# The sort back to edge order in 16-bit keys, in a graph layer with gated experts on one Trainium2 core

## The chip, the core and the metric

The kernel is one program on one core of a Trainium2 chip. The metric is the device's time for one execution, in microseconds. The engines are named as in the profile: PE (matmuls; PEld its weight loads), DVE (the vector engine), ACT (activations), POOL (here mostly the issuing of indirect DMAs), SP (issues the other DMAs).

## What is computed

The part of the reference that matters here, with the rest in a line each:

```
# x: 12500 x 256; src: 212500 edges in order of dst; edge_attr: 212500 x 32
time_feat = relu(edge_attr @ W_time.T + b_time)          # 64 features an edge
sums   = segment_sum(time_feat, src, num_segments=n)
counts = segment_sum(ones, src, num_segments=n)
node_time_feat = sums / maximum(counts, 1)[:, None]
fused = relu(concatenate([node_feat, node_time_feat]) @ W_fusion.T + b_fusion)
x = x + xn + fused @ W_up.T + b_up      # xn = layernorm(x)
x = x + ffn(layernorm(x))      # a shared MLP and the best two of four experts
```

The sums over edges by `src` are the irregular part: the edges come in the order of another index.

## The kernel before

The edges, padded to 212,992, are cut into groups of 256 (`G`), a group into 2 tiles of 128. 104 groups (`GROUPS_A_SET`) make a set, 8 sets the whole. Nodes lie in 49 buckets of 256. The main loop has 208 steps of 4 groups each. In a step PE computes the features of the step's edges (line 670), takes off with ACT's help their bf16 parts (lines 688 and 1592), and moves each group's rows with six matmuls against a one-hot matrix (line 684) into the order of the buckets, three rows of one bucket to a block. ACT copies the blocks into one of nine row buffers (line 1598), and POOL scatters them with an indirect DMA into a table in DRAM (line 1798), four in a step. A row buffer is free again when its scatter has landed. The one-hot matrix is made on DVE by line 1330 from `codes`, which give each edge of a group its slot; three buffers let DVE run ahead. When a part of the table is full (a quarter of the sets), SP loads it back, DVE makes one-hots of the nodes (line 1212), PE sums (line 713) and DVE adds to `sums` (line 1232); for the first three parts this runs in later steps of the loop, for the last after it. Then the dense layers follow for all nodes.

The slot of an edge is found by a sort on DVE. It is done for 104 groups at a time, one group a partition, and for the sets of `SETS_OF_SORT = (1, 1, 2, 2, 2)` side by side: sorts 0 and 1 have one set, sorts 2, 3 and 4 two. `sort_step(b, i)` writes step `i` of sort `b`. The first pass is a sorting network of 36 stages (`NST`) over 16-bit keys, the bucket in the upper eight bits and the edge's place in the group in the lower. Each stage is two instructions of `exchange` (lines 1130 and 1131). The middle part (`MIDDLE`, lines 1150 to 1188) finds with two scans a set each key's rank in its bucket, `turn` = rank mod 3, and the row, a count of up to `RG` = 118. The second pass is the same network over 32-bit floats, place x 1024 + turn x RG + row, and brings the edges back to their order. The last step (line 1194) takes the place off; what is left is the code:

```
elif i < SORT_STEPS - 1:
    q = i - NST - len(MIDDLE)
    exchange(q, v(f[q % 2]), v(f[(q + 1) % 2]), n)
else:
    after_op()
    op(e.tensor_tensor(v(t[0]), v(f[NST % 2]), b3d(idx_key, G, n), ALU.subtract))
```

PE transposes the codes (line 661, `turn_codes`) and ACT writes them out (line 1604). `after_op` waits until all earlier instructions of the sort have finished.

Sort 0 runs ahead of the loop, from 8.35 us on, each of its steps in turn with a bucket count (line 1106) or a step of the sizes (`size_step`, lines 913 to 1028). The other four run inside the loop: `sort_windows` gives the steps, (1, 20), (22, 46), (51, 98) and (103, 150), and `sort_at` spreads the sort's steps over them by work numbers (`NARROW_WORK`, `MIDDLE_WORK`, `WIDE_WORK`, `LAST_WORK`). In a step of the loop DVE's stream has a turn of the table, then the one-hots of the next step (lines 1322 and 1330), statistics of nodes (lines 1361 to 1375), the sort's steps and the counts.

## Time and profile before

| | |
|---|---|
| median of 3 runs | 2190.01 us (2188.02 to 2191.96) |
| the profiled execution, its own time | 2190.82 us |
| its span in the profile | 2189.0 us |
| PE busy | 2015.0 us (92%) |
| DVE busy | 1743.9 us (80%) |
| ACT busy | 1314.0 us (60%) |
| POOL busy | 1133.9 us (52%) |
| granted clock of PE over the span | 0.97 |

The span is the time from the first to the last instruction on the core. A DVE instruction's record overlaps the start of the next one by some 0.08 us, so what an instruction takes of the stream is read from start to start. The loop's first one-hot starts at 64.91 us, the first scatter at 69.6, the last at 1383.2.

### The profile page before, as it was taken

The numbers are of one execution on the slowest core, as the hardware profiler recorded it, in microseconds if no ns is written. First come the engines' busy times: TensorE is split into PE (matmuls) and PEld (weight loads), VectorE is DVE, ScalarE is ACT, GpSimd is POOL, SyncE is SP. The second block draws the span as 40 slices with busy tenths as digits, with TensorE's granted clock in tenths as the row PEclk, the third lists the DMA queues.
The fourth block names the chain that finished last, engine by engine and source line by source line (L and its number), as shares of the span: only waits on it lengthen the run. The fifth ranks groups of instructions, "written<-read, shape, count | busy, mean of one in ns | idle before, by whom it ended". The sixth has DMA issues, their size and how long they took to land.

```text
span 2189.0 us, 74658 instructions
## 1 busy us (share of the span) xinstructions
PE 2015.0 (92%) x26946; PEld 1684.2 (77%) x26946; DVE 1743.9 (80%) x5353; ACT 1314.0 (60%) x2811; POOL 1133.9 (52%) x915
## 2 busy tenths in 40 slices
PE   4789888899999899999999999687879999999998
PEld 1577676798889799999899999677756766666666
DVE  9888998888887799998687777588976776767675
ACT  2588788888788777778877787100014444444443
POOL 0587888778887878887777777200011111111110
PEclk7799999999999999999999999899989999999999
DMA  2244334676676677777678877577741121211111
GB/s 84 73 123 129 124 122 127 186 210 195 195 205 178 179 221 212 215 217 218 187 223 235 251 222 206 160 192 197 205 118 44 44 65 44 65 44 64 46 51 33
DMA packets 239404, 323.63 MB, mean 148 GB/s; under 512 B 42144, under 2 KB 213965, under 8 KB 238706
## 3 DMA queue, kind: packets, MB, share of 16 engines
q1 hardware_dynamic: 176564, 192.90, 33.4%
q0 software_dynamic: 41504, 103.41, 13.1%
q10 hardware_dynamic: 20970, 22.54, 3.8%
q8 instruction: 218, 3.57, 0.7%
q14 instruction: 148, 1.21, 0.2%
HBM read 186.34 MB, written 175.77 MB: 165 GB/s over the span
## 4 chain that ended last, share of the span: by engine, by line
PE 68%; DVE 10%; DMA 7%; ACT 6%; issue 5%; SPq 2%; DVEq 1%; POOL 1%; ACTq 1%; POOLq 0%
PE moved L684 15%; PE bank L713 14%; PE bank L800 9%; PE bank L670 7%; PE moved L813 7%; PE bank L688 4%; DMA arena<-table 3%; DMA table<-arena 3%; PE bank L840 2%; ACT arena L1598 2%; DVE arena L1130 2%; DVE arena L1330 2%; ACT arena L1592 2%; PE bank L697 1%; DVE arena L1131 1%
## 5 line engine op out<-in xcount | busy, mean ns | idle before, releaser
L1798 POOL DMA_INDIRECT table<-arena x832 | 1035.0, 1244 | 328.5 <-issue 267.4
L1598 ACT ACTIVATE arena<-moved 128x588 bf16<-128x588 f32 x832 | 546.5, 662 | 150.9 <-PE moved L684 120.6
L684 PE MATMUL moved<-arena 128*128 128x196 bf16 x4992 | 593.6, 255 | 7.0 <-ACT arena L1598 6.1
L684 PEld LDWEIGHTS moved<-arena 128*128 128x128 f16 x4992 | 455.3, 98 | 82.7 <-ACT arena L1598 18.8
L1592 ACT ACTIVATE arena<-bank 128x512 f32<-128x512 f32 x624 | 372.4, 597 | 151.5 <-PE bank L670 134.1
L1232 DVE TENSOR_TENSOR sums<-sums,bank 128x130 f32 x816 | 231.6, 284 | 156.2 <-PE bank L713 136.3
L1330 DVE TENSOR_TENSOR arena<-arena 128x2832 f16<-128x2832 f16 x208 | 338.0, 1625 | 18.0 <-PE moved L684 11.2
L713 PE MATMUL bank<-arena 128*128 128x64 bf16 (+1 forms) x7344 | 277.6, 193 | 31.9 <-DVE sums L1232 16.7
L713 PE MATMUL bank<-arena,w_all 128*128 128x64 bf16 (+1 forms) x7344 | 280.3, 194 | 19.5 <-DVE sums L1232 15.6
L713 PEld LDWEIGHTS bank<-arena 128*128 128x128 bf16 x7344 | 258.6, 98 | 36.7 <-DVE arena L1212 31.0
L713 PEld LDWEIGHTS bank<-arena,w_all 128*128 128x128 bf16 x7344 | 261.1, 98 | 24.4 <-DVE w_all L1212 17.7
L1700 ACT ACTIVATE arena<-bank,w_all 128x512 f32<-128x512 f32 (+1 forms) x225 | 152.6, 679 | 206.3 <-PE bank L800 115.5
L1212 DVE TENSOR_TENSOR arena<-arena 128x768 bf16<-128x768 bf16 x408 | 224.3, 551 | 30.4 <-DMA arena<-table 29.8
L1814 POOL TENSOR_TENSOR arena<-arena 128x4 f32<-128x4 f32 (+1 forms) x25 | 25.2, 1006 | 423.6 <-DVE arena L1503 423.6
L670 PE MATMUL bank<-w_all,arena 97*128 97x192 f32 (+1 forms) x1248 | 235.7, 326 | 4.6 <-ACT arena L1592 3.7
L1212 DVE TENSOR_TENSOR w_all<-arena 128x768 bf16<-128x768 bf16 x408 | 224.1, 551 | 10.6 <-DMA arena<-table 9.8
L800 PE MATMUL bank<-held,w_high 128*128 128x512 f32 (+1 forms) x600 | 221.0, 418 | 0.9 <-ACT arena L1700 0.5
L670 PEld LDWEIGHTS bank<-w_all,arena 97*128 97x128 f32 x1248 | 201.2, 193 | 6.7 <-issue 4.7
L688 PE MATMUL bank<-arena,minus_ident 128*128 128x512 bf16 x416 | 170.7, 410 | 38.2 <-ACT arena L1592 37.6
L1805 POOL TENSOR_TENSOR arena<-arena,w_all 128x1024 f32<-128x1024 f32 (+1 forms) x25 | 57.6, 2303 | 270.8 <-DMA arena<-x_ln 234.3
L1713 ACT ACTIVATE arena<-bank 128x256 f32<-128x256 f32 x25 | 9.4, 376 | 236.7 <-PE bank L827 236.7
L813 PE MATMUL moved<-w_all,arena 128*128 128x256 f32 x588 | 142.2, 384 | 0.0
(287 smaller groups left out, 2652.1 us busy)
## 6 DMA issues: line engine op xcount, KB each, us to landing
arena<-table SPq DMA_DIRECT2D x672, 147.0 KB
arena<-in_attr SPq DMA_DIRECT2D x208, 144.0 KB
arena<-table ACTq DMA_DIRECT2D x144, 147.0 KB
table<-arena POOLq DMA_INDIRECT x832
x_ln<-arena SPq DMA_DIRECT2D x98, 128.0 KB
arena<-in_x SPq DMA_DIRECT2D x97, 128.0 KB
arena<-x_ln SPq DMA_DIRECT2D x24, 512.0 KB, 4.7
out_rows<-arena SPq DMA_DIRECT2D x24, 512.0 KB, 3.2
```

What stands on the lines that cost most here:

```text
L670: mm = e.matmul(bank[ZB][:, q * 3 * A:q * 3 * A + w], attr_in[s % NATTR][0:ONES_AT + 1, q, :], wt[:, 0:w], start=q == 0, stop=True, skip_g ...
L684: mm = e.matmul(moved8[:, 4 * (n % 2) + h, 0:PW], slot_all[s % NSLOT][:, t * SLOTS + h * RG:t * SLOTS + h * RG + P], upper(s, 0, PW)[:, t, ...
L688: return e.matmul(z, minus_ident[:], upper(s, c0, A), start=False, stop=True, skip_group_check=True)
L713: mm = e.matmul(ps[:, v * SW:v * SW + w], one_hot, tab[t % NTB][:, c, r, c0 + at:c0 + at + w], start=i == 0 and at == 0, stop=i == CR * BL ...
L800: mm = e.matmul(bank[BH[(u - 1) % 2]][:, 0:w], weight(a, k), yt_halves[b][:, k, 0:w], start=i == 0, stop=i == len(terms) - 1)
L813: mm = e.matmul(half(BO, t), lhs[:, t * P:(t + 1) * P], rhs, start=first and t % 2 == 0, stop=done, skip_group_check=True)
L1212: e.tensor_tensor(in_pairs(hot[t % 2][:, c * PIECE:(c + 1) * PIECE]), pairs(iota_lo, PIECE), each_pair(lo_of, NODES_A_BUCKET), ALU.is_equa ...
L1232: e.tensor_tensor(d, d, sum_bank(t, c), ALU.add).then_inc(s_added, 1)
L1330: e.tensor_tensor(in_pairs(slot_hot[s % NSLOT]), pairs(iota_16, TS), each_pair(code8, SLOTS), ALU.is_equal).then_inc(s_slot, 1)
L1592: return e.activation(part_of_pay(s, c0, A), z, ACT.Relu)
L1598: e.activation(row_buf[n % NROWS], moved8[:, 4 * (n % 2):4 * (n % 2) + 3, 0:PW], ACT.Copy).then_inc(s_rows, 1)
L1798: e.indirect_dma_start(out=table, out_offset=bass.IndirectOffsetOnAxis(ap=dest[s % NDEST][:, a:a + 1], axis=0), in_=row_buf[n % NROWS].rea ...
```

## The change

The second pass gets 16-bit keys and runs on the same two buffers as the first. A key is the place x 256 + turn x 64 + the row, less 64 where the row is above 64: the row's seventh bit is left out. In the first pass's order rows only grow, so the largest first key whose row is at most 64 (`last_low`, one a set, found with a reduction) is a threshold: in the last step every edge whose first key lies above it gets its 64 back. The middle part works in 16-bit types, and its shifts and masks take two keys in a 32-bit word, the mask cutting off what came from the neighbour. The number of instructions in `middle_ops` grows by 3, that of the last step from 1 to n + 4. The work numbers and the windows are as before, so the steps of the sort stand where they stood.

```diff
@@ -216,7 +216,9 @@
         lo = carve([ET], bf16)
         codes = carve([NGR, GT, 2], f16)
         keys = [carve([G, n], u16, GP) for n in SETS_OF_SORT]
-        idx_key = carve([G], f32, GP)
+        idx_key = carve([G], u16, GP)
+        idx_16 = carve([G], f16, GP)
+        last_low = carve([max(SETS_OF_SORT)], f32, GP)
         NGM, NCM = max(ng), max(listed)
         FIRST = parts[0][1] * TS
         cnt_i = carve([NGM], i32)
@@ -247,8 +249,14 @@
         started = carve([NCM], bf16)
         SM = max(SETS_OF_SORT)
         sort_u = [carve([G * SM], u16, GP) for _ in range(2)]
-        sort_f = [carve([G * SM], f32, GP) for _ in range(2)]
-        sort_t = [carve([G * SM], f32, GP) for _ in range(2)]
+        sort_code = carve([G * SM], f32, GP)
+        bucket_16, key_16 = (sort_code.bitcast(u16)[:, i * G * SM:(i + 1) * G * SM] for i in range(2))
+        third_16 = bucket_16
+        high_16 = carve([G * SM], u16, GP)
+        LOWER = 64
+        whole_16 = carve([G * SM], u16, GP)
+        flag_16, rank_16, row_16, turn_16 = (carve([G * SM], f16, GP) for _ in range(4))
+        start_16 = row_16
         sort_zero = zeros_row[0:GP, 0:G]
         attr_in = [carve([3, P], f32) for _ in range(NATTR)]
         pay = [carve([TS, PW], f32) for _ in range(NPAY)]
@@ -394,10 +402,10 @@
 
         def middle_ops(b):
             n = SETS_OF_SORT[b]
-            return (2, 3, n, 2, 2, 2, n, 2)
+            return (1, 3, n, 2, 2, 2, n, 6)
 
         def sort_ops(b):
-            return 4 * NST + sum(middle_ops(b)) + 1
+            return 4 * NST + sum(middle_ops(b)) + SETS_OF_SORT[b] + 4
 
         def sort_no(b):
             return sum(sort_ops(q) for q in range(b))
@@ -656,7 +664,7 @@
             def turn_codes(b, q):
                 e.wait_ge(s_sort, sort_no(b + 1))
                 n = SETS_OF_SORT[b]
-                code = sort_t[0][:, 0:G * n].rearrange("p (i s) -> p i s", s=n)
+                code = sort_code[:, 0:G * n].rearrange("p (i s) -> p i s", s=n)
                 for j in range(GT):
                     mm = e.transpose(bank[MB][:, j * GP:(j + 1) * GP], code[:, j * P:(j + 1) * P, q], ident[0:GP, 0:GP])
                 mm.then_inc(s_code_ps, 1)
@@ -1140,58 +1148,73 @@
                 def v(t):
                     return t[:, 0:m].rearrange("p (i s) -> p i s", s=n)
 
-                idx3 = b3d(idx_f, G, n)
-                u, f, t = sort_u, sort_f, [*sort_t, sort_f[0]]
-                t0i, t1i, t2i, f1i = (flat(q).bitcast(i32) for q in (t[0], t[1], t[2], f[1]))
+                def two(t):
+                    return flat(t).bitcast(i32)
+
+                def both(bits):
+                    return bits << 16 | bits
+
+                idx3 = b3d(idx_16, G, n)
+                u = sort_u
+                done = u[(NST - 1) % 2]
                 if i == 0 and b:
                     e.wait_ge(s_code_ps, sort_cuts[b])
                 if i < NST:
                     exchange(i, keys[b] if i == 0 else v(u[(i - 1) % 2]), v(u[i % 2]), n)
                 elif i == NST:
                     after_op()
-                    op(e.tensor_copy(t0i, flat(u[(NST - 1) % 2])))
+                    op(e.tensor_scalar(two(bucket_16), two(done), SH, both(G - 1), ALU.arith_shift_right, ALU.bitwise_and))
+                elif i == NST + 1:
                     after_op()
-                    op(e.tensor_scalar(t1i, t0i, SH, None, ALU.arith_shift_right))
-                elif i == NST + 1:
-                    t1v = v(t[1]).bitcast(i32)
+                    op(e.memset(v(flag_16)[:, 0, :], 0.0))
+                    op(e.tensor_tensor(v(flag_16)[:, 1:G, :], v(bucket_16)[:, 1:G, :], v(bucket_16)[:, 0:G - 1, :], ALU.not_equal))
                     after_op()
-                    op(e.memset(v(f[1])[:, 0, :], 0.0))
-                    op(e.tensor_tensor(v(f[1])[:, 1:G, :], t1v[:, 1:G, :], t1v[:, 0:G - 1, :], ALU.not_equal))
-                    after_op()
-                    op(e.tensor_tensor(v(t[1]), v(f[1]), idx3, ALU.mult))
+                    op(e.tensor_tensor(v(rank_16), v(flag_16), idx3, ALU.mult))
                 elif i == NST + 2:
                     after_op()
                     for q in range(n):
-                        op(e.tensor_tensor_scan(v(f[1])[:, :, q], v(t[1])[:, :, q], sort_zero, 0.0, ALU.max, ALU.add))
+                        op(e.tensor_tensor_scan(v(start_16)[:, :, q], v(rank_16)[:, :, q], sort_zero, 0.0, ALU.max, ALU.add))
                 elif i == NST + 3:
                     after_op()
-                    op(e.tensor_tensor(v(t[1]), idx3, v(f[1]), ALU.subtract))
+                    op(e.tensor_tensor(v(rank_16), idx3, v(start_16), ALU.subtract))
                     after_op()
-                    op(e.tensor_scalar(f1i, flat(t[1]), 171.0, None, ALU.mult))
+                    op(e.tensor_scalar(flat(whole_16), flat(rank_16), 171.0, None, ALU.mult))
                 elif i == NST + 4:
                     after_op()
-                    op(e.tensor_scalar(t2i, f1i, 9, None, ALU.arith_shift_right))
+                    op(e.tensor_scalar(two(third_16), two(whole_16), 9, both(0x7F), ALU.arith_shift_right, ALU.bitwise_and))
                     after_op()
-                    op(e.scalar_tensor_tensor(flat(f[1]), t2i, -float(BLOCK), flat(t[1]), ALU.mult, ALU.add))
+                    op(e.scalar_tensor_tensor(flat(turn_16), flat(third_16), -float(BLOCK), flat(rank_16), ALU.mult, ALU.add))
                 elif i == NST + 5:
                     after_op()
-                    op(e.tensor_scalar(flat(t[2]), flat(f[1]), 0.0, None, ALU.is_equal))
-                    op(e.tensor_scalar(t0i, t0i, G - 1, None, ALU.bitwise_and))
+                    op(e.tensor_scalar(flat(flag_16), flat(turn_16), 0.0, None, ALU.is_equal))
+                    op(e.tensor_scalar(two(key_16), two(done), both(G - 1), None, ALU.bitwise_and))
                 elif i == NST + 6:
                     after_op()
                     for q in range(n):
-                        op(e.tensor_tensor_scan(v(t[1])[:, :, q], v(t[2])[:, :, q], sort_zero, 0.0, ALU.add, ALU.add))
+                        op(e.tensor_tensor_scan(v(row_16)[:, :, q], v(flag_16)[:, :, q], sort_zero, 0.0, ALU.add, ALU.add))
                 elif i == NST + 7:
                     after_op()
-                    op(e.scalar_tensor_tensor(flat(t[2]), flat(f[1]), float(RG), flat(t[1]), ALU.mult, ALU.add))
+                    op(e.tensor_scalar(flat(flag_16), flat(row_16), float(LOWER), None, ALU.is_gt))
+                    op(e.scalar_tensor_tensor(flat(rank_16), flat(turn_16), float(LOWER), flat(row_16), ALU.mult, ALU.add))
                     after_op()
-                    op(e.scalar_tensor_tensor(flat(f[0]), t0i, 1024.0, flat(t[2]), ALU.mult, ALU.add))
+                    op(e.scalar_tensor_tensor(flat(whole_16), flat(flag_16), 0.0, flat(done), ALU.is_equal, ALU.mult))
+                    op(e.scalar_tensor_tensor(flat(turn_16), flat(flag_16), -float(LOWER), flat(rank_16), ALU.mult, ALU.add))
+                    after_op()
+                    op(e.tensor_reduce(last_low[:, 0:n], flat(whole_16).rearrange("p (i s) -> p s i", s=n), AX.X, ALU.max))
+                    op(e.scalar_tensor_tensor(flat(u[0]), flat(key_16), float(G), flat(turn_16), ALU.mult, ALU.add))
                 elif i < SORT_STEPS - 1:
                     q = i - NST - len(MIDDLE)
-                    exchange(q, v(f[q % 2]), v(f[(q + 1) % 2]), n)
+                    exchange(q, v(u[q % 2]), v(u[(q + 1) % 2]), n)
                 else:
                     after_op()
-                    op(e.tensor_tensor(v(t[0]), v(f[NST % 2]), b3d(idx_key, G, n), ALU.subtract))
+                    for q in range(n):
+                        op(e.tensor_scalar(v(flag_16)[:, :, q], keys[b][:, :, q], last_low[:, q:q + 1], float(LOWER), ALU.is_gt, ALU.mult))
+                    op(e.tensor_tensor(v(whole_16), v(u[NST % 2]), b3d(idx_key, G, n), ALU.subtract))
+                    after_op()
+                    op(e.tensor_scalar(two(high_16), two(whole_16), LOWER.bit_length() - 1, both(3), ALU.arith_shift_right, ALU.bitwise_and))
+                    op(e.tensor_tensor(flat(rank_16), flat(whole_16), flat(flag_16), ALU.add))
+                    after_op()
+                    op(e.scalar_tensor_tensor(flat(sort_code), flat(high_16), float(RG - LOWER), flat(rank_16), ALU.mult, ALU.add))
                     assert sorted_ops[0] == sort_no(b + 1)
 
             regs = [e.alloc_register(f"column{i}") for i in range(CL)]
@@ -1264,7 +1287,8 @@
             e.tensor_scalar(end_id[:], iota_col[:], float(NV), float(CHUNKS), ALU.is_equal, ALU.mult)
             e.wait_ge(s_parity, 2)
             e.tensor_copy(parity[:], parity_i).then_inc(s_parity, 1)
-            e.tensor_scalar(idx_key, idx_f, 1024.0, 1.0, ALU.mult, ALU.add)
+            e.tensor_scalar(idx_key, idx_f, float(G), 1.0, ALU.mult, ALU.add)
+            e.tensor_copy(idx_16, idx_f)
             e.tensor_copy(idx_i, idx_f).then_inc(s_narrow, 1)
             e.wait_ge(s_narrow, 3)
             e.memset(pick_bucket[:, P - 2:P], 1.0)
```

The order of DVE's instructions at two places, with the semaphore that a row waits on. The first is the last step of the middle part of sort 0 ("places"), between two bucket counts (line 1106, after the change line 1114). Before:

```order
L1106 TENSOR_SCALAR arena<-arena 128x416 [waits s_bucket_ps]
L1183 SCALAR_TENSOR_TENSOR arena<-arena,held 104x256 [waits s_sort]
L1106 TENSOR_SCALAR arena<-arena 128x416 [waits s_bucket_ps]
L1186 SCALAR_TENSOR_TENSOR arena<-arena 104x256 [waits s_sort]
L1188 SCALAR_TENSOR_TENSOR arena<-arena 104x256 [waits s_sort]
L1106 TENSOR_SCALAR arena<-arena 128x416 [waits s_bucket_ps]
L1130 TENSOR_TENSOR arena<-arena 104x128 [waits s_sort]
L1131 TENSOR_TENSOR arena<-arena 104x128
```

In the changed kernel, where the exchanges are lines 1138 and 1139:

```order
L1114 TENSOR_SCALAR arena<-arena 128x416 [waits s_bucket_ps]
L1194 SCALAR_TENSOR_TENSOR arena<-arena,held 104x256 [waits s_sort]
L1114 TENSOR_SCALAR arena<-arena 128x416 [waits s_bucket_ps]
L1197 TENSOR_SCALAR arena<-arena 104x256 [waits s_sort]
L1198 SCALAR_TENSOR_TENSOR arena<-arena 104x256
L1200 SCALAR_TENSOR_TENSOR arena<-arena 104x256 [waits s_sort]
L1201 SCALAR_TENSOR_TENSOR arena<-arena 104x256
L1203 TENSOR_REDUCE arena<-arena 104x1 [waits s_sort]
L1204 SCALAR_TENSOR_TENSOR arena<-arena 104x256
L1114 TENSOR_SCALAR arena<-arena 128x416 [waits s_bucket_ps]
L1138 TENSOR_TENSOR arena<-arena 104x128 [waits s_sort]
L1139 TENSOR_TENSOR arena<-arena 104x128
```

Two instructions have become six, in three groups that wait for each other, ahead of the same bucket count. The second place is the end of sort 0, between the size steps that lead to the lists (the last of them line 1012, after the change line 1020). Before:

```order
L1130 TENSOR_TENSOR arena<-arena 104x128 [waits s_sort]
L1131 TENSOR_TENSOR arena<-arena 104x128
L1002 CAST arena<-arena 128x208 [waits s_size]
L1194 TENSOR_TENSOR arena<-arena 104x256 [waits s_sort]
L1005 TENSOR_TENSOR arena<-arena 128x208 [waits s_size]
L1007 CAST arena<-bank5 128x1
L1010 TENSOR_TENSOR arena<-bank5,arena 128x1 [waits s_size]
L1012 TENSOR_SCALAR arena<-arena 128x1
```

In the changed kernel:

```order
L1138 TENSOR_TENSOR arena<-arena 104x128 [waits s_sort]
L1139 TENSOR_TENSOR arena<-arena 104x128
L1010 CAST arena<-arena 128x208 [waits s_size]
L1211 TENSOR_SCALAR arena<-arena 104x256 [waits s_sort]
L1212 TENSOR_TENSOR arena<-arena 104x256
L1214 TENSOR_SCALAR arena<-arena 104x128 [waits s_sort]
L1215 TENSOR_TENSOR arena<-arena 104x256
L1217 SCALAR_TENSOR_TENSOR arena<-arena 104x256 [waits s_sort]
L1013 TENSOR_TENSOR arena<-arena 128x208 [waits s_size]
L1015 CAST arena<-bank5 128x1
L1018 TENSOR_TENSOR arena<-bank5,arena 128x1 [waits s_size]
L1020 TENSOR_SCALAR arena<-arena 128x1
```

The one subtraction of line 1194 has become five instructions in three groups, and the size steps behind it are the same.

## Rows read from the trace of the kernel before

**Rows 1.** The scatters on POOL: part 5 of the page; line 1798, ns min/median/max.
```profile
L1798 POOL DMA_INDIRECT table<-arena x832 | 1035.0, 1244 | 328.5 <-issue 267.4
...
L1798 POOL DMA_INDIRECT table<-arena x832: 967/1032/5419, 69.6 to 1383.2; - x167
```

**Rows 2.** Busy time of each engine in five stretches of the loop.
```profile
core 0: us, PE busy (x) PEld busy (x) DVE busy (x) ACT busy (x) POOL busy (x), PEclk, DMA share, GB/s
204.00:265.00 61.00, 51.77 (x501) 42.77 (x501) 55.25 (x180) 49.14 (x110) 48.89 (x40) 0.97 0.40 125
277.00:345.00 68.00, 60.02 (x588) 50.15 (x585) 62.21 (x177) 56.10 (x127) 55.51 (x42) 0.97 0.41 124
386.00:500.00 114.00, 108.69 (x1641) 98.03 (x1639) 97.71 (x243) 97.64 (x219) 90.84 (x77) 1.00 0.70 199
513.00:665.00 152.00, 147.06 (x2367) 135.71 (x2366) 127.94 (x304) 122.19 (x273) 121.82 (x100) 0.98 0.70 198
...
845.00:1008.00 163.00, 162.93 (x2933) 153.04 (x2932) 151.77 (x371) 128.19 (x283) 132.43 (x100) 1.00 0.76 214
```

**Rows 3.** Timeline of DVE in sort 0: start us, us, instruction. Three stages.
```profile
24.07 0.22 DVE L1130 TENSOR_TENSOR arena<-arena 104x128 uint16<-104x128 uint16 x1
...
24.34 0.26 DVE L1106 TENSOR_SCALAR arena<-arena 128x416 bf16<-128x416 bf16 x1
...
24.97 0.30 DVE L1130 TENSOR_TENSOR arena<-arena 104x128 uint16<-104x128 uint16 x1
...
32.57 0.28 DVE L1130 TENSOR_TENSOR arena<-arena 104x128 f32<-104x128 f32 x1
...
32.98 0.26 DVE L1106 TENSOR_SCALAR arena<-arena 128x416 bf16<-128x416 bf16 x1
```

**Rows 4.** Timeline from the end of sort 0 to the loop, all engines.
```profile
56.02 0.42 DVE L1194 TENSOR_TENSOR arena<-arena 104x256 f32<-104x256 f32 x1
...
56.90 0.14 DVE L1012 TENSOR_SCALAR arena<-arena 128x1 f32<-128x1 f32 x1
...
64.91 1.63 DVE L1330 TENSOR_TENSOR arena<-arena 128x2832 f16<-128x2832 f16 x1 [6.55 <-ACT arena L1604]
```

**Rows 5.** Timeline, 16-bit stages of two sets on DVE, issues on POOL, one one-hot.
```profile
204.65 0.98 POOL L1798 DMA_INDIRECT table<-arena  x1 [0.30 <-ACT arena L1598]
...
221.67 0.29 DVE L1130 TENSOR_TENSOR arena<-arena 104x256 uint16<-104x256 uint16 x1
...
222.20 0.29 DVE L1130 TENSOR_TENSOR arena<-arena 104x256 uint16<-104x256 uint16 x1
...
225.15 1.63 DVE L1330 TENSOR_TENSOR arena<-arena 128x2832 f16<-128x2832 f16 x1
225.62 2.00 POOL L1798 DMA_INDIRECT table<-arena  x1 [0.30 <-issue]
...
781.78 0.97 POOL L1798 DMA_INDIRECT table<-arena  x1 [0.30 <-issue]
```

**Rows 6.** Timeline, 32-bit stages of two sets on DVE, issues on POOL.
```profile
276.54 1.05 POOL L1798 DMA_INDIRECT table<-arena  x1 [0.31 <-issue]
...
917.09 0.42 DVE L1130 TENSOR_TENSOR arena<-arena 104x256 f32<-104x256 f32 x1
...
917.88 0.43 DVE L1130 TENSOR_TENSOR arena<-arena 104x256 f32<-104x256 f32 x1
...
994.92 1.16 POOL L1798 DMA_INDIRECT table<-arena  x1 [0.31 <-issue]
```

**Rows 7.** Groups of DVE instructions by line and shape: us busy, mean ns of one.
```profile
L1186 DVE SCALAR_TENSOR_TENSOR arena<-arena 104x512 f32<-104x512 f32 x3 | 2.1, 687 | 0.0
L1154 DVE TENSOR_SCALAR arena<-arena 104x512 int32<-104x512 int32 x3 | 1.5, 488 | 0.1
L1154 DVE TENSOR_SCALAR arena<-arena 104x256 int32<-104x256 int32 x2 | 0.6, 296 | 0.1
...
L1322 DVE TENSOR_TENSOR arena<-arena 128x512 f16<-128x512 f16 x208 | 86.8, 418 | 1.2 <-issue 1.0
```

## The prediction

> **What bounds the kernel.** I read first which engine has no slack in the loop, then what slows that engine, and only then what the change saves. Line 1798 is the 832 indirect DMAs by which POOL scatters the rows into the table; they run from 69.6 to 1383.2 us [rows 1]. POOL was idle 328.5 us before them. Of that 67.1 us lie ahead of the first; the other 261.4 fall on 831 gaps, 0.31 us each, and the gap between two issues that wait for nothing is 0.30 already [rows 5]. So in 1314 us of loop POOL waited some 12 us, though its share of the whole span is only 52%. An issue takes 0.967 us at its shortest and 1.244 on the mean [rows 1]; the excess over all is 832 x 0.277 = 230 us.
>
> The table of stretches [rows 2] sets the other engines beside it. It takes sort 2 in its 16-bit and its 32-bit pass (from 204 and from 277), sort 3 (386 and 513), and the 32-bit pass of sort 4 (845). DVE is busy 84 to 93% of each, never all; PE 85 and 88% in the first two, 95 and 97% in the next, and 162.9 of 163 us in the last, at full granted clock. So I read: POOL paces the loop to about 720 us, PE from about 760, where POOL and PE run nearly level. DVE sets the pace only ahead of the loop, where it runs without a gap [rows 3].
>
> **How DVE reaches POOL.** An issue beside the 1.63 us one-hot instruction of line 1330 does not finish until 0.84 us after that one's end: the one-hot started at 225.15 and ended at 226.78, the issue that began at 225.62 took 2.00 and ended at 227.62 [rows 5]. The sort does the same on a smaller scale: issues beside 32-bit exchanges of two sets took 1.05 and 1.16 us [rows 6], issues beside 16-bit ones 0.98 and 0.97, the minimum [rows 5]. The same shows in the stretches. POOL's busy time over its count is 48.89/40 = 1.222 (16 bits) against 55.51/42 = 1.322 (32 bits) for sort 2, and 90.84/77 = 1.180 against 121.82/100 = 1.218 for sort 3 [rows 2].
>
> **The change, part by part.**
>
> 1. *The 36 stages of the second pass, of two instructions each, go from 32 to 16 bits.* For one set, ahead of the loop, a stage takes 32.98 - 32.57 = 0.41 us in 32 bits and 24.34 - 24.07 = 0.27 in 16 [rows 3]. The 8 stages of distance 1 gain nothing: their 16-bit instructions take 0.30 each (24.97) where the 32-bit ones take 0.28. So 28 x 0.14 = 3.8 us. For two sets, in the loop, a stage takes 917.88 - 917.09 = 0.79 [rows 6] against 222.20 - 221.67 = 0.53 [rows 5]: 36 x 0.26 = 9.4 us for each of three sorts. Sort 1 (one set, in the loop) gets about what sort 0 gets.
>
> 2. *The middle and the last step grow.* The four scans stay. Counted for two sets, 13 other instructions become 21. Before: 7 of two inputs at 0.687 (the form of line 1186) and 6 of one input at 0.488 (line 1154, 512 elements) [rows 7] make 7.7 us. After: 9 of one input at 0.296, the time that line 1154 takes for 256 words, since the shifts now take two keys in a word; 2 plain 16-bit tensor_tensor at 0.418 (line 1322, 512 elements); and 10 others: six scalar_tensor_tensor, three with an operand repeated over the sets, one reduction. No row shows these ten in 16 bits. At the 16-bit pace they take 0.418, at the 32-bit pace 0.687: the whole is 2.7 + 0.8 + 4.2 = 7.7 or 2.7 + 0.8 + 6.9 = 10.4. I take 0.687, because the nearest row, the same operation on the same shape (line 1186), runs at it. That is 2.7 us more a sort of two sets, between 0 and 2.7; for one set half, 1.3. The Trainium skill (Vector Engine (DVE) Microarchitecture Reference, section 5.1) lists copies, casts, tensor_scalar and tensor_tensor for the packed 16-bit mode, with elements side by side, and not scalar_tensor_tensor; it stands on the side of 0.687, and no run here shows it yet. By 0.418 the part ahead of the loop would be 1.3 us better.
>
> 3. *Ahead of the loop.* The order excerpt at the end of sort 0 shows five instructions where one stood, in front of the size steps. DVE's stream from there to line 1012 (56.90), PE's matmuls for the lists, the features, the transposed codes and the first one-hot at 64.91 follow each other [rows 4]. All of it moves by what DVE gains: 3.8 - 1.3 = **2.5 us**.
>
> 4. *In the loop, by POOL.* For sorts 2 and 3, if the 32-bit stretches take on the 16-bit pace: 42 x 0.100 = 4.2 and 100 x 0.038 = 3.8, together 8.0. From single issues: 49 lie beside 32-bit exchanges of two sets and not beside a one-hot (the first at 276.54, the last at 994.92), 0.18 above 0.967 on the mean [rows 6]; 30 beside 16-bit ones (204.65 to 781.78), 0.02 to 0.03 [rows 5]. Of the 49, 32 belong to sorts 2 and 3: 32 x 0.155 = 5.0. Between 5.0 and 8.0 I take the middle, **6.5 us**. The eight added instructions of each middle part cost some tenths of this and lie within it.
>
> 5. *In the loop, sorts 1 and 4.* The 32-bit instructions of sort 1 have one set each, 0.28 us like those of sort 0 [rows 3], and two of them hold an issue no longer than one 16-bit pair of two sets; I take 0. Sort 4 runs where PE has no gap: 0, though POOL alone would give 100 x 0.057 = 5.7. What covers the cost of the middle parts here is DVE's idle share, 7% in that stretch [rows 2]; without it they would cost up to 2.7 us a sort.
>
> Sum: 2.5 + 6.5 = 9.0 us. The profiled execution took 2190.8 us (span 2189.0) and gives 2181.8; it lay 0.8 above the median of 2190.0, so **2181 us**. A measurement of this kernel can tell about 0.2% (4.4 us) from no change.
>
> **Rivals.**
>
> *DVE counts in full.* If the loop stood still wherever DVE works, the gain would be 3 x (9.4 - 2.7) + 2 x (3.8 - 1.3) = 25.1 us: 2165. For it speaks that DVE is busy 91% in two of the stretches and 93% in the last. Against it: POOL does not wait [rows 1]. Chance 0.13.
>
> *Only the part ahead of the loop counts.* POOL would be held as long as before by 16-bit pairs, or PE would take over at once: 2.5 us, 2187.5. For it: PE is at 97% in the stretch at 513. Against it: the 0.97 of rows 5. Chance 0.22. The Trainium skill (GPSIMD Engine Reference, Key points) says that GpSimd contends for its memory interfaces with DVE instructions of two SBUF inputs, which the 16-bit pairs have as well. By that rule, a rival of its own inside this one, the hold would shrink only as the pair's time, 0.79 to 0.53: from the 32 x 0.18 = 5.8 us of the singles a third is 1.9, and with the 2.5 the time is 2185.6. The 0.03 over 30 issues speaks against it; of the 0.22 it gets 0.07.
>
> *Slower, by the one-hots.* An issue that asks at the start of a one-hot's 1.63 us is held for all of it, one that asks 1.27 later (0.967 and the gap, the least distance of two issues) for 0.36. So one step's hold can be anywhere from 0.36 to 1.63; 195 issues end 0.84 us after a one-hot's end, as the one of rows 5 does, and hold 161 us of the 230, 0.78 for each of 208 one-hots. The change moves DVE's stream against POOL's. Over some 100 steps that POOL paces, a mean of 0.98 costs 20 us, 11 more than is gained: 2201. It decides from 0.78 + 9.0/100 = 0.87 on. For it: nothing ties the two streams. Against it: they drift over many steps, which averages it. Chance 0.13.
>
> *The change does not do what it says*, if the second pass kept the 32-bit pace. The first pass already runs such exchanges on the same two buffers at the 16-bit pace, which speaks against it. It would leave the 1.3 us of the middle part ahead of the loop: 2191.3. Chance 0.02.
>
> **The numbers.** Forecast 0.50, full gain 0.13, only ahead 0.22, slower 0.13, not done 0.02. The drift of the one-hots spreads each case by some 5 us either way. Faster by over 0.2% (below 2185.6): most of the forecast, 0.42, the full gain, 0.13, and a part of the second, 0.07: 0.62. Slower (above 2194.4): 0.11. Same: 0.27. The range, 2167 to 2192, leaves out the far half of the full gain and most of the slower case.
>
> **What would show it.** In the profile after: 16-bit exchanges x432 of two sets and none in 32 bits; the six scalar_tensor_tensor at 0.69 for 512 elements; the first one-hot at 62.4 instead of 64.91; POOL's busy time an issue near 1.22 for sort 2 and 1.18 for sort 3 in their second passes; the last scatter at about 1374 instead of 1383.2. The forecast is wrong if the first one-hot moves and the last scatter does not move further (then the holds were not the sort's), if the stretch from 845 shortens too (then PE was not the bound there), or if the mean hold beside the one-hots has moved.

## The result, and the profile after

The changed kernel takes 2177.74 us (median of 16 runs, 2168.52 to 2187.74), the kernel before beside it 2191.32 (16 runs, 2184.84 to 2199.39): a ratio of 0.9937 [0.9922, 0.9951], 13.8 us less. A repeat on another chip gave 2179.65 against 2190.20, 0.9948 [0.9926, 0.9969]; weighted by runs the two make 0.9941, **12.9 us**. Forecast were 9.0. Single runs of one kernel lie up to 13 us from their median, so two single traces can't tell a few us; where it matters, several traces are put together below.

The profiled execution took 2171.82 us, its span is 2170.0. The scatters of [rows 1], now line 1822, from part 5 of the page and from the view of the line:

```profile
L1822 POOL DMA_INDIRECT table<-arena x832 | 1007.8, 1211 | 337.1 <-issue 263.3
...
L1822 POOL DMA_INDIRECT table<-arena x832: 967/1022/3369, 67.5 to 1365.3; - x167
```

The mean issue fell from 1244 to 1211 ns. The first scatter moved by 2.1 us, the last by 17.9. The stretches of [rows 2], shifted to the same work (columns as there):

```profile
203.00:263.00 60.00, 50.35 (x500) 42.12 (x499) 54.41 (x177) 48.18 (x109) 48.41 (x39) 0.99 0.40 127
275.00:343.00 68.00, 58.92 (x584) 49.98 (x584) 55.90 (x179) 55.78 (x125) 52.11 (x46) 0.97 0.43 131
384.00:500.00 116.00, 109.91 (x1670) 98.14 (x1668) 97.78 (x248) 99.14 (x222) 92.82 (x77) 1.00 0.69 198
508.00:655.00 147.00, 146.86 (x2441) 135.98 (x2440) 123.61 (x315) 126.56 (x282) 116.52 (x101) 1.00 0.74 212
830.00:991.00 161.00, 161.00 (x2927) 150.92 (x2926) 144.55 (x372) 127.84 (x283) 129.86 (x103) 1.00 0.77 218
```

The two first passes (203, 384) stand where they stood. In the three second passes POOL is busy 52.11/46 = 1.133 us an issue (before 1.322), 116.52/101 = 1.154 (1.218) and 129.86/103 = 1.261 (1.324). The time of the stretch over its issues fell as well: 1.478 (1.619), 1.455 (1.520), 1.563 (1.630). The last line looks like a surprise, since no gain was forecast for sort 4. The table of PE's steps below says how much of it is one.

DVE's instructions by line and shape (us busy, mean ns of one, as in [rows 7]):

```profile
L1139 DVE TENSOR_TENSOR arena<-arena 104x256 uint16<-104x256 uint16 x216 | 62.0, 287 | 0.0
L1138 DVE TENSOR_TENSOR arena<-arena 104x256 uint16<-104x256 uint16 x216 | 61.5, 285 | 4.6
...
L1211 DVE TENSOR_SCALAR arena<-arena 104x256 f16<-104x256 uint16 x8 | 2.9, 405 | 0.1
L1212 DVE TENSOR_TENSOR arena<-arena 104x512 uint16<-104x512 uint16 x3 | 2.1, 711 | 0.0
L1172 DVE TENSOR_TENSOR arena<-arena 104x512 f16<-104x512 f16 x3 | 2.1, 692 | 0.1
...
L1203 DVE TENSOR_REDUCE arena<-arena 104x2 f32<-104x512 uint16 x3 | 2.1, 686 | 0.1
L1198 DVE SCALAR_TENSOR_TENSOR arena<-arena 104x512 f16<-104x512 f16 x3 | 2.0, 682 | 0.0
L1184 DVE TENSOR_SCALAR arena<-arena 104x256 int32<-104x256 int32 x3 | 1.3, 428 | 0.0
L1170 DVE TENSOR_TENSOR arena<-arena 104x510 f16<-104x510 uint16 x3 | 1.3, 421 | 0.0
```

All exchanges have 16 bits. The plain tensor_tensor (1170) runs at 0.42; scalar_tensor_tensor, the reduction and a tensor_tensor with an operand repeated over the two sets (1172, 1212) run at 0.68 to 0.71, though every element has 16 bits. And the end of sort 0, of [rows 4]:

```profile
53.95 0.42 DVE L1217 SCALAR_TENSOR_TENSOR arena<-arena 104x256 f32<-104x256 uint16 x1
...
54.85 0.14 DVE L1020 TENSOR_SCALAR arena<-arena 128x1 f32<-128x1 f32 x1
...
62.86 1.63 DVE L1354 TENSOR_TENSOR arena<-arena 128x2832 f16<-128x2832 f16 x1 [6.56 <-ACT arena L1628]
```

The sort's last instruction starts 2.07 us earlier, the first one-hot 2.05 earlier.

**By steps of the loop.** Each step has four scatters, so step n begins with scatter 4n. Starts of the scatters 136, 184, 296, 396, 500 and 608 (steps 34, 46, 74, 99, 125, 152), first before:

```profile
289.95 1.20 POOL L1798 DMA_INDIRECT table<-arena  x1 [0.30 <-issue]
...
366.88 0.97 POOL L1798 DMA_INDIRECT table<-arena  x1 [0.30 <-issue]
...
537.55 1.57 POOL L1798 DMA_INDIRECT table<-arena  x1 [0.30 <-issue]
...
692.56 1.58 POOL L1798 DMA_INDIRECT table<-arena  x1 [0.30 <-issue]
...
856.48 1.16 POOL L1798 DMA_INDIRECT table<-arena  x1 [0.31 <-ACT arena L1598]
...
1032.12 1.57 POOL L1798 DMA_INDIRECT table<-arena  x1 [0.31 <-ACT arena L1598]
```

and after:

```profile
287.28 1.28 POOL L1822 DMA_INDIRECT table<-arena  x1 [0.89 <-ACT arena L1622]
...
361.95 1.07 POOL L1822 DMA_INDIRECT table<-arena  x1 [0.30 <-ACT arena L1622]
...
532.83 1.03 POOL L1822 DMA_INDIRECT table<-arena  x1 [0.30 <-issue]
...
681.19 2.21 POOL L1822 DMA_INDIRECT table<-arena  x1 [0.30 <-issue]
...
846.10 1.16 POOL L1822 DMA_INDIRECT table<-arena  x1 [0.30 <-ACT arena L1622]
...
1013.76 1.16 POOL L1822 DMA_INDIRECT table<-arena  x1 [0.30 <-ACT arena L1622]
```

Steps 34 to 46 (sort 2's second pass) went from 76.9 to 74.7 us, 74 to 99 (sort 3's) from 155.0 to 148.4, 125 to 152 (sort 4's) from 175.6 to 167.7. The same differences in every trace ("pieces" are the experiments on the one-hot, below):

```
us of the steps                34-46   46-74   74-99   125-152   152-207   last scatter at
before                          76.9   170.7   155.0   175.6     347.2     1383.2
changed                         74.7   170.9   148.4   167.7     347.7     1365.3
changed, again (e5)             73.5   174.8   149.9   172.1     351.1     1373.9
sort 0 old (e1)                 75.2   170.8   154.6   169.1     351.9     1377.8
sorts 2 and 3 old (e2)          77.6   174.2   159.2   170.4     347.0     1379.8
sort 4 old (e3)                 74.7   171.9   151.2   178.4     347.6     1376.7
4 copies a stage (e4)           76.1   175.3   151.4   171.8     348.5     1381.8
8 copies a stage (e8)           80.8   169.6   155.3   177.4     349.9     1392.0
changed, four pieces (e6)       75.2   164.0   143.6   169.6     347.2     1356.8
changed, two pieces (e7)        74.8   168.0   149.7   172.0     346.2     1365.3
four pieces from step 46 (e9)   74.9   166.7   142.5   169.7     345.8     1352.6
e9, other work numbers (e11)    71.7   166.1   147.2   173.6     346.8     1356.3
before, four pieces (e10)       75.3   164.7   145.4   173.5     347.9     1366.3
```

A scatter starts 2.2 us behind PE's matmuls of its rows at the least and up to 17 us behind them when POOL has a backlog. So a stretch that is read from scatters holds the change of the backlog as well. The same steps by PE, each from the first matmul of the rows of its first step, together with two sums over all 832 issues: what they took above 0.967 us each ("held"), and POOL's idle time beyond its gap of 0.30 us ("waits"):

```
us of the steps on PE          34-74   74-99  99-125  125-152  152-207    held   waits
before                         241.4   155.2   170.7   174.8    348.1    230.4    12.2
changed                        239.9   147.5   165.9   173.5    347.3    203.3    22.8
changed, again (e5)            240.6   152.6   167.2   173.5    348.2    214.8    22.7
sort 0 old (e1)                239.1   153.3   167.9   173.5    347.5    209.9    28.5
sorts 2 and 3 old (e2)         241.4   162.9   165.8   173.5    346.6    222.3    17.6
sort 4 old (e3)                240.0   151.2   166.1   176.0    350.5    221.1    15.2
4 copies a stage (e4)          242.2   153.1   169.3   175.3    349.8    227.8    15.5
8 copies a stage (e8)          242.4   155.5   170.7   175.4    354.1    231.7    23.1
changed, four pieces (e6)      234.7   147.2   162.4   173.5    346.8    149.9    69.6
changed, two pieces (e7)       236.4   147.5   168.9   173.5    345.8    179.8    45.2
four pieces from step 46 (e9)  233.6   149.8   162.2   173.5    345.5    157.7    57.6
e9, other work numbers (e11)   232.4   148.7   168.0   173.4    346.5    163.5    55.6
before, four pieces (e10)      235.5   148.2   163.5   174.6    347.5    165.9    60.9
```

PE's rows at steps 125 and 152 of the kernel before:

```profile
853.68 0.70 PE L684 MATMUL moved<-arena 128*128 128x196 bf16 x6
854.23 0.40 PE L688 MATMUL bank<-arena,minus_ident 128*128 128x512 bf16 x1
...
1028.51 0.70 PE L684 MATMUL moved<-arena 128*128 128x196 bf16 x6
1029.05 0.40 PE L688 MATMUL bank<-arena,minus_ident 128*128 128x512 bf16 x1
```

and of the changed one:

```profile
837.86 0.69 PE L692 MATMUL moved<-arena 128*128 128x196 bf16 x6
838.38 0.39 PE L696 MATMUL bank<-arena,minus_ident 128*128 128x512 bf16 x1
...
1011.33 0.69 PE L692 MATMUL moved<-arena 128*128 128x196 bf16 x6
1011.85 0.39 PE L696 MATMUL bank<-arena,minus_ident 128*128 128x512 bf16 x1
```

Two things follow. In steps 125 to 152 PE takes 173.4 or 173.5 us in all eight traces that have the new sort 4 and no copies, while their scatters take 167.7 to 173.6. In the first trace of the change POOL came into the stretch 8.2 us behind PE and left it 2.4 behind, so 5.8 of the 7.9 us by which the scatters' stretch is shorter are backlog. And the matmuls of the rows are themselves faster in the changed kernel: from the first of the six to the next instruction it is 0.52 us instead of 0.55, at the same granted clock of 1.00. Over each trace the first and the sixth start 0.452 us apart at the median in the kernel before and in e10, and 0.438 or 0.439 in all the others, those with old sorts too. So the sort's instructions don't make this difference. What these kernels share is the layout: `last_low` adds two words, and the buffers carved behind it lie 8 bytes further in SBUF (32 or 1024 more with the copies and with an old sort). That this is the cause was not tried. It is a part of the change that the theory below does not have.

### The profile page after: what moved, and what is told of

It is laid out like the page before. It is cut to its first block, busy times and chain, and to the rows that moved or that the text cites. A ratio compares the mean times of both kernels' runs of the same rounds, so it can differ in the third digit from the quotient of the medians.

```text
span 2170.0 us, 74697 instructions
## 1 busy us (share of the span) xinstructions
PE 1999.9 (92%) x26946; PEld 1670.0 (77%) x26946; DVE 1722.2 (79%) x5392; ACT 1313.0 (61%) x2811; POOL 1107.5 (51%) x915
## 4 chain that ended last, share of the span: by engine, by line
PE 70%; DVE 10%; DMA 6%; ACT 5%; issue 4%; POOL 1%; DVEq 1%; SPq 1%; ACTq 1%; POOLq 0%
PE moved L692 15%; PE bank L721 15%; PE bank L808 10%; PE bank L678 7%; PE moved L821 7%; PE bank L696 4%; DMA arena<-table 3%; DMA table<-arena 2%; PE bank L848 2%; ACT arena L1622 2%; ACT arena L1616 2%; PE bank L705 2%; DVE arena L1354 2%; DVE arena L1138 1%; PE bank L640 1%
## 5 line engine op out<-in xcount | busy, mean ns | idle before, releaser
L1822 POOL DMA_INDIRECT table<-arena x832 | 1007.8, 1211 | 337.1 <-issue 263.3
L692 PE MATMUL moved<-arena 128*128 128x196 bf16 x4992 | 576.7, 251 | 6.0 <-ACT arena L1622 4.7
L692 PEld LDWEIGHTS moved<-arena 128*128 128x128 f16 x4992 | 444.9, 97 | 79.9 <-ACT arena L1622 18.4
L1354 DVE TENSOR_TENSOR arena<-arena 128x2832 f16<-128x2832 f16 x208 | 338.4, 1627 | 18.7 <-PE moved L692 12.0
```

The lines of the kernel that those rows point to most:

```text
L692: mm = e.matmul(moved8[:, 4 * (n % 2) + h, 0:PW], slot_all[s % NSLOT][:, t * SLOTS + h * RG:t * SLOTS + h * RG + P], upper(s, 0, PW)[:, t, ...
L1354: e.tensor_tensor(in_pairs(slot_hot[s % NSLOT]), pairs(iota_16, TS), each_pair(code8, SLOTS), ALU.is_equal).then_inc(s_slot, 1)
L1822: e.indirect_dma_start(out=table, out_offset=bass.IndirectOffsetOnAxis(ap=dest[s % NDEST][:, a:a + 1], axis=0), in_=row_buf[n % NROWS].rea ...
```

## The experiments

My theory: POOL paces the loop, and the sort reaches it by the time for which its 32-bit pairs hold an issue. Its rivals: DVE's time itself counts; or only the start counts and the rest is chance. A third, the faster matmuls of the rows, was seen only in the kept traces.

**Undo one sort at a time.** `sort_step_wide` is the old `sort_step` with 32-bit buffers of its own; with OLD_SORTS = (0,), (2, 3) or (4,):

```diff
+                if b in OLD_SORTS:
+                    return sort_step_wide(b, i)
```

> The changed kernel with sort 0 alone (ahead of the loop) in its old form. By every theory the first one-hot goes back to about 64.9 us and the time rises by the 2.0 us by which the change moved it: about 2180, ratio to the kernel before 0.9946. If the start is worth more or less than its shift, the time says so.

Measured: 2181.69 against 2192.43, 0.9953 [0.9926, 0.9981]. The first one-hot is back where it was (0.4 us later than before's). Against the change's 0.9941 that is 2.6 us, the size of the term, but inside the interval.

> Sorts 2 and 3 in their old form, sorts 0, 1 and 4 as changed. Holds of POOL: nearly the whole gain in the loop is lost, 8 to 12 us, time 2186 to 2190, ratio 0.997 to 1.000; last scatter about 1375 to 1381 instead of 1365.3. Chance (the profiled pair differed by where long waits fell): the time stays within 3 us of 2178.

Measured: 2187.86, 0.9977 [0.9962, 0.9992]: 7.9 us are lost, with an uncertainty of some 4. In both tables the loss lies in the steps of these two sorts, most of it in sort 3's (162.9 us on PE in steps 74 to 99), and those of sort 4 keep their 173.5.

> Sort 4 alone in its old form. PE bounds its stretch: time within 2 us of the changed kernel, 2177 to 2180, ratio 0.993 to 0.995. If DVE's time counts there, 6.7 us are lost: 2184. If POOL's holds count there, up to 5.7: 2183.

Measured: 2181.19, 0.9955 [0.994, 0.997]: 3.1 us are lost, which the timed interval alone would not decide. The steps point the same way, by less than the scatters say: the scatters of 125 to 152 take 178.4 us against 167.7 to 172.1 in the four traces with the new sort 4, but PE takes 176.0 against 173.5, and 350.5 against 347.4 in the steps behind it. So sort 4 gave a few us, against the 0 of my step 5. The three parts sum to 2.6 + 7.9 + 3.1 = 13.6 us, the whole gain within its interval; the start alone explains a fifth. All three kernels have the fast matmuls of the rows, so these parts are the sort's own. As each is known to some 4 us only, the sum does not exclude that the matmuls gave some of the 12.9 too.

> The changed kernel once more, beside the other three on the same chip, for a second trace. Ratio 0.992 to 0.996. If the step times of the second pass are the change's own, sort 3's second pass takes 5.93 to 6.03 us a step again and sort 2's 6.2; if the first trace was lucky, nearer 6.2 and 6.4.

Measured: 2179.65, 0.9948 [0.9926, 0.9969]. Sort 3's second pass took 149.9/25 = 6.00 us a step and sort 2's 73.5/12 = 6.1, so these are the change's own. The trace ends the scatters at 1373.9, 8.6 us after the first trace of the same kernel: half of the 17.9 us that the first pair of traces shows is the drift of the streams.

**DVE's time back, without the 32-bit pairs.** Small copies of one column (0.14 us each, one input) after each second-pass stage of sorts 2, 3 and 4:

```diff
                     exchange(q, v(u[q % 2]), v(u[(q + 1) % 2]), n)
+                    if b in (2, 3, 4):
+                        for j in range(4):
+                            op(e.tensor_copy(idle_cols[:, j:j + 1], iota_col[0:GP]))
```

> The changed kernel, and after each stage of the second pass of sorts 2, 3 and 4 four copies of one column, which give DVE back the 0.25 us that the stage had lost but with nothing long that could hold POOL. Holds of POOL: the gain stays, 2177 to 2181, ratio 0.994 to 0.9955. DVE's time: the gain in the loop goes, 2188 to 2190, ratio 0.9985 or more.

Measured: 2185.11, 0.9966 [0.9952, 0.9979], 5.5 us lost, between the two forecasts. DVE's busy time rose by 24.8 us, to 1747.0, about what the change had taken away, and less than half of the gain went with it.

> As the kernel with four copies a stage, with eight: DVE's time is now above the kernel before's by some 30 us over sorts 2, 3 and 4. Holds of POOL: little more is lost than with four, ratio 0.996 to 0.998. DVE's time in proportion: twice the loss of the four, 13 us above the changed kernel, ratio 0.9995 or more.

Measured: 2201.18, 1.0047 [1.0027, 1.0066]. DVE's busy time rose by 46.1 us, to 1768.3, and 23 us were lost: the first 24.8 cost 5.5, the next 21.3 cost 18. DVE's time is neither free nor counted in full.

The two runs do not set DVE's time apart from the holds, as they were meant to. The copies hold next to nothing: the issues beside copies and 16-bit exchanges, with no one-hot or 512-element instruction near, took 0.02 us above the minimum with four copies (49 issues) and 0.03 with eight (51). But the issues that overlap a one-hot took 189.6 us above it in sum with four copies and 201.6 with eight, against 170.2 and 181.3 in the two traces of the change (189.7 before). So "held" in the table is 228 and 232, nearly the 230 of the kernel before, while POOL waited no more than in the changed kernel: most of the loss is issues held longer by the one-hots. Why more one-input work moves issues under the one-hots is open. In one place the loss is DVE's time itself.

That place is the end of sort 2. There line 962 (a step of the list sizes) ends DVE's queue of sort work, PE waits for it in line 647 ahead of the matmuls of the rows, ACT's row copy (1622) waits for those and POOL for the copy. Timeline of the changed kernel:

```profile
350.47 0.97 POOL L1822 DMA_INDIRECT table<-arena  x1 [0.30 <-issue]
...
350.87 0.16 DVE L962 TENSOR_TENSOR arena<-arena,even_col 128x1 bf16<-128x1 f32 x1
...
351.08 0.59 PE L647 MATMUL bank<-arena,below 128*128 128x1 f32 x2 [4.47 <-DVE arena L962]
...
354.04 0.66 ACT L1622 ACTIVATE arena<-moved 128x588 bf16<-128x588 f32 x1 [6.18 <-PE moved L692]
...
355.56 0.97 POOL L1822 DMA_INDIRECT table<-arena  x1 [4.12 <-ACT arena L1622]
```

of the kernel before, where PE waits as long, but POOL was so far behind that it did not notice:

```profile
353.02 0.15 DVE L954 TENSOR_TENSOR arena<-arena,even_col 128x1 bf16<-128x1 f32 x1
...
353.23 0.59 PE L639 MATMUL bank<-arena,below 128*128 128x1 f32 x2 [4.01 <-DVE arena L954]
...
353.91 1.22 POOL L1798 DMA_INDIRECT table<-arena  x1 [0.30 <-issue]
...
355.43 1.24 POOL L1798 DMA_INDIRECT table<-arena  x1 [0.30 <-issue]
```

and of the one with eight copies:

```profile
357.30 0.15 DVE L963 TENSOR_TENSOR arena<-arena,even_col 128x1 bf16<-128x1 f32 x1
...
357.51 0.59 PE L648 MATMUL bank<-arena,below 128*128 128x1 f32 x2 [7.73 <-DVE arena L963]
...
361.99 0.97 POOL L1826 DMA_INDIRECT table<-arena  x1 [7.57 <-ACT arena L1626]
```

POOL waits 0.30 (its issue gap), 4.12 and 7.57 us. In the changed kernel DVE is the bound at this point. Over the steps 34 to 46 the excess of the issues over 0.967 us fell from 1.32 to 0.59 us a step, 8.8 us, and POOL's waits beyond its gap rose by 6.5 us, 3.8 of them here. In sort 4 the eight copies cost 8 us by the scatters (177.4 against a mean of 169.8 for the new sort; on PE 2 us there and 7 in the steps behind) with hardly a wait of POOL; there the issues are held longer beside the one-hots (1.03 us a step against 0.79 in the first trace of the change and 0.64 to 0.80 in the three others with the new sort 4).

**The holds alone, with more DVE work.** If long two-input instructions hold POOL, the largest lever is the one-hot. Cut into four pieces it is the same computation in more instructions:

```diff
-                e.tensor_tensor(in_pairs(slot_hot[s % NSLOT]), pairs(iota_16, TS), each_pair(code8, SLOTS), ALU.is_equal).then_inc(s_slot, 1)
+                for j in range(4):
+                    t0, t1 = TS * j // 4, TS * (j + 1) // 4
+                    ins = e.tensor_tensor(in_pairs(slot_hot[s % NSLOT][:, t0:t1]), pairs(iota_16, t1 - t0), each_pair(code8[:, t0:t1], SLOTS), ALU.is_equal)
+                ins.then_inc(s_slot, 1)
```

> The changed kernel with each one-hot instruction cut into four of a quarter of its size. Holds of POOL: an issue then waits for a quarter at most, the mean hold of a one-hot falls from 0.71 us to 0.2 or 0.3, POOL gets faster by some 0.4 us a step where it paces, until PE bounds at 95 to 97%: 10 to 25 us better, 2153 to 2168, ratio 0.983 to 0.989. If POOL only gets in when DVE's whole sequence is over: the hold stays, and 208 x 3 x 0.07 = 44 us more of DVE's time make it the same or slower, 0.994 to 1.002. If DVE's time bounds the loop: slower than the changed kernel by 10 us or more.

Measured: 2162.24, 0.9877 [0.9854, 0.99]. Page of that kernel:

```profile
L1825 POOL DMA_INDIRECT table<-arena x832 | 954.5, 1147 | 384.1 <-issue 257.2
...
L1356 DVE TENSOR_TENSOR arena<-arena 128x708 f16<-128x708 f16 x832 | 381.4, 519 | 15.2 <-PE moved L692 8.5
```

The pieces cost DVE 381.4 us where the whole ones took 338.4 (208 x 1.627), 43 more, and the kernel is 14 us faster than the change: the mean issue fell by 64 ns. This is what separates the theories: more DVE time, shorter instructions, less time. Issues still wait for a piece and get in before the next: of the 182 issues beside pieces that took over 1.05 us, 118 end 0.82 to 0.88 us after a piece's end, and for 101 of these it is not the last piece.

> As the one in four, in two halves. Holds of POOL: mean hold some 0.4 us, about half to three quarters of the other's gain, 2160 to 2172. Else as there with a third of the added DVE time.

Measured: 2167.50, 0.989 [0.9869, 0.9912], mean issue 1183 ns: two pieces (0.889 us each) give less than four, though the intervals meet.

> The kernel before (32-bit second pass) with one-hots in four pieces in all steps. Holds of POOL alone: the pieces gain what they gain on the changed kernel, 13 us, and the sort's change is still worth its 13: 2176, ratio 0.993 to 0.995. If DVE's time counts once it is short (the kernel with eight copies a stage suggests it): the pieces' 44 us and the second pass's 31 us together push DVE over its limit, and the ratio is 0.997 or more. If the holds by the sort and by the one-hots overlap, so that one relief gives most of both: 0.988 to 0.991.

Measured: the kernel before with four pieces takes 2170.42, 0.991 [0.9887, 0.9933]. So the pieces are worth 20 us without the sort's change and 14 with it, and the change 7 us with the pieces and 13 without. That they take the same holds away would give such a difference, but 6 us lie within the uncertainty of these four figures, some 7, and it is not shown. Of the 7 us that are left of the change, 2.1 are the start, and 1.1 lie in steps 125 to 152, where PE waits for nothing in either kernel (174.6 against 173.5), which the faster matmuls of the rows account for.

> The changed kernel with one-hots in four pieces, from step 46 of the loop on only; the steps before it gained nothing from the pieces in the trace (6.27 us against 6.2 for steps 34 to 46, 7.40 against 7.2 for steps 0 to 8), since DVE has no time to spare there. Expected 1 to 5 us below the kernel with pieces everywhere: ratio 0.985 to 0.988.

The edit is `pieces = 4 if s >= 46 else 1`, since in e6 the steps before 46, where DVE has no slack, had gained nothing: over steps 0 to 34 the holds fell by 4.4 us and POOL's waits rose by 5.2. Measured: **2157.98** against 2189.09, 0.9847 [0.9822, 0.9872], 31 to 33 us less than the kernel before and the lowest median of all. Its interval meets that of e6 (0.9854 to 0.99), so that it is better to leave the early steps whole is likely and not shown. Timeline of its steps, four pieces in one row:

```profile
602.63 1.19 POOL L1826 DMA_INDIRECT table<-arena  x1 [0.30 <-ACT arena L1626]
602.89 1.84 DVE L1357 TENSOR_TENSOR arena<-arena 128x708 f16<-128x708 f16 x4
604.13 1.01 POOL L1826 DMA_INDIRECT table<-arena  x1 [0.30 <-ACT arena L1626]
```

The pieces run from 602.89 to 604.73, and the two issues beside them take 1.19 and 1.01 us instead of the 2.00 of [rows 5]. Neither waited for all four: the first ends while the pieces run, at 603.82, and the second, at 605.14, 0.41 us after the fourth's end and not 0.84.

> As the kernel with pieces from step 46 on, with the work numbers that spread the sort over the steps set to the measured durations (second pass 3 as the first instead of 4, the last step of the middle part 18 instead of 7, the last step 13 instead of 4). Within 3 us of it either way; better by 1 to 3 if uneven steps cost time.

Measured: 2158.92, 0.9852 [0.9828, 0.9876], the same as e9 as far as the intervals tell, and they could not show the 1 to 3 us.

## Why the prediction was right, and where it was wrong

The direction held, and the mechanism in the main. The size was a third short: 9.0 us were forecast and 12.9 came, with single terms off by up to 3 us.

1. *Second pass in 16 bits*: right (x216 of two sets at 0.285 and 0.287). For sort 0 the sum had a slip (28 x 0.14 is 3.9, not 3.8).
2. *The middle*: the choice of 0.687 for the ten unknown instructions was right (six scalar_tensor_tensor, three repeated operands and the reduction took 0.68 to 0.71). Two that I had as cheap were dearer: line 1184 takes 0.428 on the mean and line 1211 0.405, where I had 0.296. In sum the counted instructions of a sort of two sets went from 7.6 to 10.7 us, 3.1 more, where I had 2.7. The Trainium skill (Vector Engine (DVE) Microarchitecture Reference, section 5.1) does not list scalar_tensor_tensor among the packed operations; the trace agrees (0.682 for 104x512 in f16).
3. *Ahead of the loop*: 2.05 instead of 2.5. The middle and the last step cost 1.2 us, as forecast (1.3). The second pass gave 3.4 instead of 3.8, and sort 0 starts 0.20 us later (8.55 instead of 8.35), behind the added copy to `idx_16`, which the sum did not have.
4. *Sorts 2 and 3 by the holds*, forecast 6.5: too small. Measured 7.9 by undoing them. By PE's steps 34 to 99, with the traces put together, it is 400.5 us with the old sorts (two traces) against 391.1 with the new (four), 9.4 us, of which sort 3 has most. Sort 2's share was cut by the wait for line 962. Counted over the whole loop, the excess over 0.967 us of the issues that do not end 0.84 us after a one-hot's end fell from 68.4 us to 56.0 and 55.5 (the two traces of the change). These 12 to 13 us are near the 4.2 + 3.8 + 5.7 = 13.7 that the stretches gave for sorts 2, 3 and 4. The estimate from single issues (5.0) was the worse one.
5. *Sort 4: 0, as PE has no gap*: right about PE, wrong about the 0. PE had no gap in steps 125 to 150, before or after. Its 27 steps took 174.8 us before and 173.5 after; e10, with the old sort and short holds, has 174.6. Those 1.1 to 1.3 us are what the faster matmuls of the rows account for (27 x 4 sixes, each 0.014 us shorter, make 1.5), and no step of the prediction has them. What the holds do shows in e3, which has the fast matmuls and the old sort 4: 176.0 us there and 3.1 more in the steps behind, where PE waits for ACT's row copies while POOL is 8 us behind. The timed loss of 3.1 us agrees. POOL and PE ran level here (132.43 us busy and 100 gaps of 0.30 make 162.4 of 163), and I took level for covered. The sign that I had named, a shorter stretch from 845, came up, and it does not mean what I had said: a stretch read from scatters shrinks with POOL's backlog, though PE is the bound. 173.5 us, or 6.43 a step, is PE's floor here, since holds from 150 to 222 us in sum leave it where it is. The Trainium skill (Perfetto Trace Analysis, Identifying the Most-Contended Engine) warns that matmul busy share is no good measure of how close PE is to its roofline and points to the weight loads; their share here was 153.04/163 = 0.94. The warning fits in so far as PE's busy share of 1.00 hid the 3% by which the matmuls of the rows could go faster.

So the terms that were short are the holds of sorts 2 and 3 (6.5 against 7.9 to 9.4) and those of sort 4 (0 against some 3), and the start was 0.45 us too large.

The rivals: *DVE counts in full* fell, since the copies give 24.8 us back for 5.5 and the pieces add 43 us and gain 14; it holds only where slack has ended, as at the end of sort 2. *Only ahead of the loop* fell with e2, and its version by the rule on two SBUF inputs too. *Slower by the one-hots* did not come: the hold per one-hot was 0.78 us before and 0.71 and 0.77 in the two traces of the change. But the drift that it spoke of is real, the 8.6 us between those two traces, of the size that I had put on each case, and the runs with copies lost most of their time in this way. That the change itself did not may be luck in part.

Not all of the shorter holds reached the end. They fell by 27.1 and 15.6 us in the two traces of the change, and POOL's waits beyond its gap rose in both from 12 us to 23. Which engine sets each of these waits, beside the one at 351, was not tried. By PE's steps the gains are 2.0 for the start, 9.4 for sorts 2 and 3 and 1.3 to 2.5 for steps 125 to 152, together 13 to 14 us, near the timed 13. Read from the scatters, steps 125 to 152 alone would seem to give 7.2 us, the mean of 175.6 and 178.4 against 169.8.

## What to carry to other kernels

An engine whose instructions are stretched by another's reads as "busy" and not as "waiting": compare the mean duration with the shortest one, and look for what stands beside the long ones. If that is a long two-input DVE instruction, cut it into pieces, even though DVE's total grows; where DVE had no slack (steps 0 to 34) this gave nothing. Before a stretch is given to an engine that is 100% busy, check whether another one's busy time plus its issue gaps fills the stretch as well. When two kernels are compared by stretches, take the same work on each engine: the scatters of 27 steps came 7.9 us closer, and PE's matmuls of the same steps 1.3. And when a change moves buffers, compare the duration of instructions that it does not touch.

## What the runs showed of the hardware

- An indirect DMA's issue on GpSimd waits for the running two-input DVE instruction as a whole. In the kernel before 195 issues end 0.84 us after the end of a 1.63 us one-hot, and those that overlap one take 1.51 us on the mean. With 0.46 us pieces (e6) they take 1.26. Issues beside 32-bit pairs of 0.34 us, start to start, took 0.18 above the minimum of 0.967, those beside 16-bit pairs of 0.2 us 0.02 to 0.03 [rows 5] [rows 6]. The Trainium skill (SBUF — State Buffer, A bandwidth-pool intuition that's wrong) has the same picture for a DVE `tensor_copy`, blocked until the DVE instruction ends and some 0.115 us more; the 0.84 us seen here is the rest of the issue as well, and the two were not told apart.
- Cutting 2832 elements into four pieces of 708 costs 0.21 us a one-hot in DVE's time. The Trainium skill (VectorE: DVE Perf Modes, the section on the TRN2 errata) advises tiles of 512 elements or more for this very cost. The pieces keep to that, and the trace agrees with the cost; but between 2832 and 708 the holds weigh more here, and the smaller pieces won by 14 us.
- 16-bit operands speed up a plain tensor_tensor (0.42 for 510 elements) but not one with an operand repeated over the two sets (0.69 and 0.71), nor scalar_tensor_tensor or a reduction (0.68 to 0.69).
- The holds go the other way as well, it seems. Line 1184, a shift and a mask on 256 int32 words, took 0.50, 0.29 and 0.49 us in the three sorts of two sets. Beside both long ones an issue of POOL that had begun earlier ended 0.38 us after the instruction's start. Lines 1166 and 1214, of the same form, took 0.289 and 0.321 on the mean. That the issue held the instruction was not tried.
- Six matmuls of 196 bf16 columns with the same operands took 0.452 us from the first to the last start in two kernels and 0.438 or 0.439 in all with the layout of the change, 8 bytes or more further, at a granted clock of 1.00.
